# Mamba input projections as three terms of rounded operands, with the rows and weights split into a rounded part and a remainder

## What is computed

```
xn = layernorm(x)                                   # 4 x 1024 x 256
zxbcdt = xn @ w_in                                  # 256 -> 1288 = 512 (z) + 768 (xBC) + 8 (dt)
dt = softplus(zxbcdt[..., 1280:] + dt_bias)         # 8 heads
xBC = silu(conv4(zxbcdt[..., 512:1280]) + conv_b)   # 4 taps along the sequence
y = ssd(xh * dt, dt * -exp(A_log), B, C) + xh * D
y = y * silu(z);  y = y * rsqrt(mean(y * y) + eps) * norm_w
x = x + xn + y @ w_out
```

## Time and profile before

| | |
|---|---|
| runs of the kernel before | 2184.39, 2201.05, 2202.07 us; median 2201.05 |
| profiled execution | 2185.0 us; span 2183.1 us |
| TensorE busy | 1819.3 us, 83% of the span |
| VectorE, ScalarE, GpSimd busy | 1191.3, 822.7, 725.6 us |
| Mamba stage | 1265.1 us (its first DMA issue) to about 1756 us |
| TensorE in the window 1262 to 1757 us | 430.5 us busy, mean granted clock 0.93 |

### The profile page before, as it was taken

How to read it: one execution, slowest core, us unless ns; L and a number is a source line. 1 busy time by engine, 2 the same in 40 slices (tenths; PEclk the granted TensorE clock), 3 DMA queues, 4 the chain that set the end, 5 groups by cost and what they waited for, 6 DMA issues and landing times. The chain is left out here.

```text
span 2183.1 us, 30159 instructions
## 1 busy us (share of the span) xinstructions
PE 1819.3 (83%) x9520; PEld 1212.1 (56%) x9520; DVE 1191.3 (55%) x2979; ACT 822.7 (38%) x1705; POOL 725.6 (33%) x922
## 2 busy tenths in 40 slices
PE   5368889889888864899999658989898938999997
PEld 3133334434433322788888535747484727888886
DVE  4466676666666508543443356665656685443442
ACT  2036655656665624111111035554646441111111
POOL 2335464464462312222222124333242312222221
PEclk9569989989988855999999969999999978999999
DMA  5522333332442108000000230100101080000000
GB/s 160 174 89 90 119 126 95 122 125 77 134 135 87 39 16 313 22 24 28 26 25 26 70 111 15 43 36 1 78 1 78 1 309 22 26 24 30 25 24 9
DMA packets 90179, 161.23 MB, mean 74 GB/s; under 512 B 23080, under 2 KB 50476, under 8 KB 88880
## 3 DMA queue, kind: packets, MB, share of 16 engines
q1 hardware_dynamic: 71504, 107.39, 14.7%
q0 software_dynamic: 17984, 50.62, 7.2%
q10 hardware_dynamic: 544, 1.31, 0.2%
HBM read 102.52 MB, written 45.48 MB: 68 GB/s over the span
## 5 line engine op out<-in xcount | busy, mean ns | idle before, releaser
L690 ACT ACTIVATE a_probs<-a_ps_e 128x512 f32<-128x512 f32 (+3 forms) x768 | 336.0, 491 | 204.1 <-PE a_ps_e L854 200.9
L438 DVE CUSTOM_DVE_ANT_0 a_ps_m<-a_ps_m,a_causal 128x512 f32<-128x512 f32 (+3 forms) x512 | 239.4, 517 | 97.5 <-PE a_ps_m L841 96.4
L1433 PE MATMUL g_ps_y<-g_w_d,x_res 128*128 x1120 | 253.2, 379 | 2.8 <-DVE x_res L1203 2.8
L854 PE MATMUL a_ps_e<-a_q_st,a_k_st 64*128 64x512 f32 (+3 forms) x768 | 187.9, 480 | 76.4 <-ACT a_probs L690 48.5
L854 PEld LDWEIGHTS a_ps_e<-a_q_st,a_k_st 64*128 64x128 f32 x768 | 79.6, 201 | 289.8 <-ACT a_probs L690 200.5
L1433 PEld LDWEIGHTS g_ps_y<-g_w_d,x_res 128*128 128x128 f32 x1120 | 212.3, 190 | 34.6 <-issue 3.2
L442 DVE TENSOR_REDUCE a_peak<-a_ps_m 128x1 f32<-128x512 f32 x256 | 164.8, 686 | 94.8 <-PE a_ps_m L841 94.1
L841 PE MATMUL a_ps_m<-a_k_st,a_q_st 64*128 64x512 f32 (+3 forms) x768 | 152.7, 399 | 68.8 <-DMA a_k_st<-a_scr_k 28.0
L1323 ACT COPY x_res<-g_ps_h 128x512 f32<-128x512 f32 x70 | 41.1, 587 | 439.2 <-PE g_ps_h L1441 439.2
L576 POOL TENSOR_SCALAR_AFFINE_SELECT a_probs<-a_probs 128x256 f32<-128x256 f32 x256 | 103.9, 408 | 284.1 <-ACT a_probs L690 283.8
L1170 DVE BATCH_NORM_STATS2 g_xe_stats<-x_res 128x6 f32<-128x256 f32 x70 | 29.9, 426 | 295.6 <-DMA x_res<-g_x_rows,g_token_i 295.6
(11 more groups left out here) (272 smaller groups left out, 3664.5 us busy)
## 6 DMA issues: line engine op xcount, KB each, us to landing
a_q_st<-a_scr_q POOLq DMA_DIRECT2D x32, 512.0 KB, 4.0
a_k_st<-a_scr_k POOLq DMA_DIRECT2D x32, 512.0 KB, 4.8
m_spread_acs<-m_acs_rows SPq DMA_DIRECT2D x8, 2048.0 KB, 9.7
a_scr_q<-a_high SPq DMA_DIRECT2D x36, 256.0 KB
a_scr_k<-a_high SPq DMA_DIRECT2D x36, 256.0 KB
a_swapped<-a_raw SPq DMA_DIRECT2D x64, 128.0 KB, 2.0
g_w_gu<-L_ffn_Wg SPq DMA_DIRECT2D x8, 1024.0 KB, 9.8
g_w_gu<-L_ffn_Wu SPq DMA_DIRECT2D x8, 1024.0 KB, 12.4
```

The source lines that it names most:

```text
L438: nc.vector.tensor_tensor_reduce(ps_m[:, bank, 0:w], ps_m[:, bank, 0:w], causal[:, 512 - w:], 1.0, MASKED, ALU.add, ALU.max, peak[:, p % 2 ...
L690: nc.scalar.activation(probs[:, N % RING, r, q0:], ps_e[:, (2 * N + r) % HEAD_BANKS, q0:], ACT.Exp, scale=DH ** -0.5).then_inc(exp_done, 1)
L854: nc.tensor.matmul(ps_e[:, (2 * N + r) % HEAD_BANKS, q0:], k_st[rows(r), p % BUFS, j * P:(j + 1) * P], q_st[rows(r), p % BUFS, 512 * c + q ...
L1433: last = nc.tensor.matmul(ps_y[:, 0:D], hid_t[:, f * P:(f + 1) * P], w_d[:, bass.ds(e, 1), f].rearrange("p a d -> p (a d)"), start=(f == 0 ...
```

## The change

The projections no longer multiply f32 operands. Weights and transposed rows are each held as a rounded part (`w_hi`, `xt_hi`, type F32R) and a rounded remainder (`w_lo`, `xt_lo`), and a product is the sum of three terms, hi x hi, hi x lo, lo x hi. `w_in` is loaded into the space of `spread_acs`; ScalarE rounds it, VectorE subtracts. The rows' rounded part is ScalarE's copy out of PSUM; VectorE's new `split_x` subtracts it from the bank, so the bank comes free later. `xn` holds four tiles instead of eight. In the loop `norm` runs in steps 0, 1, 3, 4, `turn_x` in 2, 3, 5, 6, `sizes` in 7; `sums` stands behind group 1 instead of group 0.

```diff
@@ mamba
-    XT_AT, DT_AT = (2, 3, 4, 5), 6
+    XT_AT, DT_AT = (2, 3, 5, 6), 7
-        w_in = sb("w_in", [P, DT, IN_PROJ])
+        w_hi = sb("w_hi", [P, DT, IN_PROJ], F32R)
+        w_lo = sb("w_lo", [P, DT, IN_PROJ], F32R)
-        xn = sb("xn", [P, T, D])
-        xn_t = sb("xn_t", [P, DT, SEQ])
+        xn = sb("xn", [P, HALF, D])
+        xt_hi = sb("xt_hi", [P, DT, SEQ], F32R)
+        xt_lo = sb("xt_lo", [P, DT, SEQ], F32R)
+        w_raw = spread_acs[:].rearrange("p t h l -> p (t h l)")[:, 0:DT * IN_PROJ].rearrange("p (t e) -> p t e", t=DT)
@@ sync
-            sp.dma_start(w_in[:], M["w_in"].rearrange("(t p) e -> p t e", p=P)).then_inc(loaded, 16)
+            sp.dma_start(w_raw, M["w_in"].rearrange("(t p) e -> p t e", p=P)).then_inc(w_loaded, 16)
                 if b >= 1:
                     sp.wait_ge(decay_ready, 2 * T * b)
+                else:
+                    sp.wait_ge(w_split, DT)
@@ vector
             def norm(b, t):
                 N = b * T + t
-                if b >= 1:
-                    dve.wait_ge(xt_ps, 4 * (b - 1) + (2 if t < HALF else 4))
-                    dve.wait_ge(xn_added, N - T + 1)
-                nc.vector.tensor_scalar(xn[:, t], X[:, N], mean_var[:, N, 0:1], rstd[:, N:N + 1], ALU.subtract, ALU.mult
+                if N >= HALF:
+                    dve.wait_ge(xt_ps, 4 * b + (0 if t < HALF else 2))
+                    dve.wait_ge(xn_added, N - HALF + 1)
+                nc.vector.tensor_scalar(xn[:, t % HALF], X[:, N], mean_var[:, N, 0:1], rstd[:, N:N + 1], ALU.subtract, ALU.mult
                                         ).then_inc(xn_ready, 1)
-            for t in range(T):
+            def split_x(b, i):
+                dve.wait_ge(xt_sb, 4 * b + i + 1)
+                some = slice(i // 2 * 512, i // 2 * 512 + 512)
+                nc.vector.tensor_tensor(xt_lo[:, i % 2, some], ps_r[:, 1], xt_hi[:, i % 2, some].bitcast(F32), ALU.subtract
+                                        ).then_inc(xt_split, 1)
+
+            for t in range(HALF):
                 norm(0, t)
-            dve.wait_ge(loaded, 16 * 9)
+            for d in range(DT):
+                dve.wait_ge(w_rounded, d + 1)
+                nc.vector.tensor_tensor(w_lo[:, d], w_raw[:, d], w_hi[:, d].bitcast(F32), ALU.subtract).then_inc(w_split, 1)
+            for i in range(2):
+                split_x(0, i)
+            for t in range(HALF, T):
+                norm(0, t)
+            for i in range(2, 4):
+                split_x(0, i)
+            dve.wait_ge(loaded, 16 * 8)
@@ vector, token loop
-                    if b + 1 < BATCH and t < HALF:
+                    if b + 1 < BATCH and t < 2:
                         norm(b + 1, 2 * t)
                         norm(b + 1, 2 * t + 1)
-                    if b + 1 < BATCH and t == DT_AT + 1:
-                        step_sizes(b + 1)
+                    if b + 1 < BATCH and t in XT_AT:
+                        split_x(b + 1, XT_AT.index(t))
+                    if b + 1 < BATCH and t in (3, 4):
+                        norm(b + 1, HALF + 2 * (t - 3))
+                        norm(b + 1, HALF + 2 * (t - 3) + 1)
+                if b + 1 < BATCH:
+                    step_sizes(b + 1)
@@ scalar
-            act.wait_ge(loaded, 16 * 9)
-            nc.scalar.activation(a_neg[:, 1], a_neg[:, 0], ACT.Exp).then_inc(act_fixed, 1)
+            act.wait_ge(w_loaded, 16)
+            for d in range(DT):
+                nc.scalar.copy(w_hi[:, d], w_raw[:, d]).then_inc(w_rounded, 1)
             for i in range(4):
                 turned_x(0, i)
+            act.wait_ge(loaded, 16 * 8)
+            nc.scalar.activation(a_neg[:, 1], a_neg[:, 0], ACT.Exp).then_inc(act_fixed, 1)
@@ tensor, turn_x
                 if i >= 1:
-                    pe.wait_ge(xt_sb, 4 * b + i)
+                    pe.wait_ge(xt_split, 4 * b + i)
@@ tensor, channels (sizes and gates alike)
+            TERMS = [(xt_hi, w_hi), (xt_hi, w_lo), (xt_lo, w_hi)]
+            PASSES = [(x, w, d, (n, d) == (0, 0), (n, d) == (2, DT - 1)) for n, (x, w) in enumerate(TERMS) for d in range(DT)]
-                    for d in range(DT):
-                        one = nc.tensor.matmul(bank[:, 0], w_in[:, d, INNER + c * P:INNER + (c + 1) * P],
-                                               xn_t[:, d, 512 * k:512 * (k + 1)], start=(d == 0), stop=(d == DT - 1))
+                    for x, w, d, first, final in PASSES:
+                        one = nc.tensor.matmul(bank[:, 0], w[:, d, INNER + c * P:INNER + (c + 1) * P],
+                                               x[:, d, 512 * k:512 * (k + 1)], start=first, stop=final)
@@ tensor, order of the projections
                     channels(b, n)
+                    if n == 1:
+                        sums(b)
                     if n == 0:
-                        sums(b)
                         if b >= 1:
                             turn_y(b * T - 1)
```

More of the change, by code:

```diff
@@ L1911, in _ @@
                         turned_x(b + 1, XT_AT.index(t))
-                    if b + 1 < BATCH and t == DT_AT + 1:
-                        sizes_exp(b + 1)
+                if b + 1 < BATCH:
+                    sizes_exp(b + 1)
             squares(NT - 1)
@@ L1924, in turn_x @@
                 if i >= 1:
-                    pe.wait_ge(xt_sb, 4 * b + i)
+                    pe.wait_ge(xt_split, 4 * b + i)
                 for t in range(HALF):
-                    one = nc.tensor.transpose(ps_r[:, 1, t * P:(t + 1) * P], xn[:, half * HALF + t, d * P:(d + 1) * P],
-                                              ident)
+                    one = nc.tensor.transpose(ps_r[:, 1, t * P:(t + 1) * P], xn[:, t, d * P:(d + 1) * P], ident)
                 one.then_inc(xt_ps, 1)
+            TERMS = [(xt_hi, w_hi), (xt_hi, w_lo), (xt_lo, w_hi)]
+            PASSES = [(x, w, d, (n, d) == (0, 0), (n, d) == (2, DT - 1)) for n, (x, w) in enumerate(TERMS) for d in range(DT)]
             def sizes(b):
-                pe.wait_ge(xt_sb, 4 * b + 4)
+                pe.wait_ge(xt_split, 4 * b + 4)
                 if b == 0:
-                    pe.wait_ge(loaded, 16 * 9)
+                    pe.wait_ge(w_split, DT)
                 for t in range(T):
-                    for d in range(DT):
-                        one = nc.tensor.matmul(ps_r[:, 1, t * MHEADS:(t + 1) * MHEADS], xn_t[:, d, t * P:(t + 1) * P],
-                                               w_in[:, d, INNER + CONV:], start=(d == 0), stop=(d == DT - 1))
+                    for x, w, d, first, final in PASSES:
+                        one = nc.tensor.matmul(ps_r[:, 1, t * MHEADS:(t + 1) * MHEADS], x[:, d, t * P:(t + 1) * P],
+                                               w[:, d, INNER + CONV:], start=first, stop=final)
                 one.then_inc(dt_ps, 1)
@@ L1959, in gates @@
                     pe.wait_ge(dt_used, b + 1)
-                for d in range(DT):
-                    one = nc.tensor.matmul(ps_r[:, t % 2], xn_t[:, d, t * P:(t + 1) * P], w_in[:, d, 0:INNER],
-                                           start=(d == 0), stop=(d == DT - 1))
+                for x, w, d, first, final in PASSES:
+                    one = nc.tensor.matmul(ps_r[:, t % 2], x[:, d, t * P:(t + 1) * P], w[:, d, 0:INNER], start=first,
+                                           stop=final)
                 one.then_inc(z_ps, 1)
```

6 lines of the change are left out of this document (3 added, 3 removed).

## The result

| | before | after |
|---|---|---|
| median | 2199.15 us (12 runs, 2183.41 to 2214.22) | 2213.8 us (12 runs, 2202.04 to 2218.89) |
| ratio of after to before | | 1.0068, 95% interval [1.0039, 1.0097] |
| profiled execution | 2185.0 us | 2208.39 us |
| span, mean granted clock | 2183.1 us, 0.901 | 2206.5 us, 0.887 |

The changed kernel is slower by 0.7%, inside the 1% that counted as no difference, and 6 us under the 2220 that was forecast. The two profiled executions are 23.4 us apart, the medians 14.7; the profiled execution of before lies at the low end of its runs. The comparison by stages uses the profiled pair.

The account below looks back on a forecast made before the run. TensorE and ScalarE take turns in the projections; TensorE bounds the token loop. Start 7.4, later sequences 0.5, clock at gate tiles 7.6 and seams 3.7 sum to 19.2 us on the median 2201.05: 2220, range 2190 to 2242.

Parts of the forecast that it names:

- The passes: Projections: rounded passes of 0.233 us, 0.316 us less per bank, 25.3 us if all 80 banks lay on the path.
- The sums: Running sums after n = 1 delay the second gate tile: 1.56 us more, 3.2 in the first sequence.
- The clock at the gate tiles: Clock falls after the new idle at the second gate tile: 1.9 us lost, four times, 7.6 us.
- The clock at the seams: Half clock right behind the step-size matmuls, at two of three seams instead of one: +3.7 us.
- The step sizes: 48 rounded eight-column passes at 0.113 us: +1.8 us in each later sequence, +3.4 in the first.
- Rival 3: Eight-column step-size pass costs as much as the wide one: +27, 2247 us; chance 0.08.
- From n = 0 to n = 1: Later projections: TensorE waits for a bank behind ScalarE's logarithm, -0.6 us instead of the full gain.
- The start: First sequence: step-size matmuls start 4.8 us later, behind weight subtractions, norms and row splits.
- The splits in the loop: Token loop: four row subtractions of 0.68 us a sequence, hidden inside VectorE's wait of 1.59 us.
- Rival 4: Token loop: the subtractions are not hidden, +16, 2236 us; chance 0.08.
- Rival 1: The clock holds and both clock terms drop out: 7.4 + 0.5, 2209 us; chance 0.22.
- Rival 2: Second gate tile does not wait, everything gained on TensorE counts: -11.6, 2190 us; chance 0.07.

Follow-up runs that it names:

- the run with the gate wait filled: Changed kernel with 16 unused rounded 512-column passes (22 in the first sequence) ahead of the second gate tile of n = 2: 2203.03 us, 1.0040.
- the one-term run: Changed kernel with only the first term of the step-size matmuls, 16 passes instead of 48: 2184.98 us, 0.9964 of the kernel before.
- the combined one: Changed kernel with sums behind group 0, 16-column step sizes, reordered start and first-sequence transposes in two PSUM banks: 2174.23 us, 0.9907 of the kernel before.

## Why the prediction was right, and where not

The forecast was 19.2 us over the kernel before. The medians are 14.7 apart and the stages of the profiled pair 20.9. The causes it named are the ones that the runs show, but the total is partly luck: the clock at the seams was forecast at half of what it costs, and smaller differences the other way made up for it. By its own terms:

*The passes.* 0.233 us each, as taken from the expert stages, and where TensorE is in the chain it gave what was said. Free of the clock's share, in the run with the gate wait filled, n = 3, 4 and 5 took 7.23, 4.19 and 11.18 against 8.21, 5.15 and 11.83: 0.98, 0.96 and 0.65 less, forecast 1.06, 0.95 and 0.63.

*The sums.* n = 1 and n = 2 together grew by 1.5 with the clock held, forecast 1.6: right. The way there was right up to the first convolution and wrong in its last links. The chain put the table load behind the convolution, since in the earlier trace rows its start and the convolution's end fall together; the changed kernel's trace has it ahead (1430.16), right behind ScalarE's evictions, so silu(0) ends 10.3 us behind S (the start of n = 1, 1425.81), not 11.35. That did not bring the gate forward, because silu(1) then waited for VectorE's second convolution (0.63 us), which the chain had left out: gate tile at S + 15.04, forecast 15.25. Two mistakes cancelled. The wait was 3.69 us, forecast 4.5, mostly because TensorE's own work up to it was 11.35, not 10.75; in the first sequence 5.03, forecast 6.1.

*The clock at the gate tiles.* Forecast 7.6, and the traces with and without filling are 7.6 apart between n = 2 and n = 4: right. The times give 6, within wide intervals. The Trainium skill ("TensorE: Matmul & The Clock Gate", section "What's actually happening") puts the ramp penalty below 1% of a typical kernel's span and advises against fitting a particular count of slow matmuls. This term is 0.3% of the span, so it alone stays within that bound; but the whole difference here is 0.7%, and this term is about half of it.

*The clock at the seams.* This is the term that was mis-sized: 3.7 in all, for one more seam of three. All three fell, each costs 3.8 by the one-term run, and the kernel before had one of them, so the term is two seams, 7.6. The fall was also put in the wrong place: it comes inside the narrow passes, not behind them as the earlier trace rows had it.

*The step sizes.* 0.111 a pass at full clock and 0.213 at half, forecast 0.113 and 0.214; the first sequence grew by 3.4, as forecast. Rival 3 falls.

*From n = 0 to n = 1.* Forecast 0.6 less a sequence. It measured 5.40, 5.68 and 5.48 against 5.13, 5.91 and 5.13, no gain, since most of that stretch ran at half clock; with the clock up it is 4.35, 0.8 less. In the first sequence it was to take 5.1 us at half clock and took 4.52, since the clock rose before its end (the passes at 1305.63 are already faster).

*The start.* Step sizes 5.0 later, forecast 4.8, by errors that cancelled: the weights' subtractions took 1.98 each, not 1.44, and the norms 0.55, not 0.64.

*The splits in the loop.* Hidden, as forecast. VectorE's wait for the diagonal, forecast near 0.2 in such a step, is 0.33 in the fifth, and behind the first the loop's steps kept their lengths (7.92 for the later ones in both kernels, one of them 7.69 in the changed kernel; 8.10 is the longest, once, in the kernel before):

```profile
1399.68 0.69 DVE L1617 TENSOR_TENSOR m_xt_lo<-m_ps_r,m_xt_hi 128x512 fp32r<-128x512 f32 x1 [0.57 <-ACT m_xt_hi L1834]
...
1402.61 0.69 DVE L1720 TENSOR_TENSOR m_y<-m_y,m_ps_y 128x512 f32<-128x512 f32 x1 [0.33 <-PE m_ps_y L2051]
```

What the profile was to show is there: the first step-size matmul at 1291.81, which is 1289.7 without the 2.1 us that lie ahead of the stage; one long wait at a gate tile in each sequence with a clock under 1 behind it, though in three of the four it is 3.69 or 3.68 and only the 5.03 of the first lies in the forecast 4.5 to 6; the second wait of each two-gate step at 1.39 to 1.40, forecast 1.5.

Rival 4 falls with the splits. Rival 1, a clock that holds, falls by the half clock behind every gate wait and in every seam, and by the filled gate wait and the one-term run, which give its price. Rival 2, everything gained on TensorE counts, is not what the changed kernel does. In the combined one 15.2 of the 25.3 us appear in the projections once the late sums are gone. Its remaining gate waits of 1.40 us, three a sequence, where the earlier trace rows have 1.07, are part of the rest.

## What to carry to other kernels

Cheaper passes on the engine that looks busiest turned into a wait, because one small step (three matmuls of running sums) had moved behind them: before a term is booked, follow the step that stands next in each other engine's program. A narrow pass costs its weight block (0.111 us with 8 columns and with 16), so columns that go through the same stationary operand should go side by side in one pass. And the waits of 3.5 to 5 us here cost more than themselves, by the half clock behind them. Useless passes in them took 7.6 us off that stretch in one kernel, and in another the clock fell later instead and the kernel's time did not move. Such a filling is therefore judged by the whole kernel's time.
